# Two PSUM banks each for the scan's scores and outputs, and one merged product for base and routing in a decoder layer

## What is computed

```python
# 1: mixer and MLP            (B, L, D = 8, 128, 512; 4 heads of 128; INTER = 1792)
h   = x + mamba2(rmsnorm(x) * ln1_w)          # in-projection, convolution, scan, out-projection
h2  = rmsnorm(h) * ln2_w
x   = layernorm(x + h + silu(h2 @ gate_w.T) * (h2 @ up_w.T) @ down_w.T)
# the scan of a tile: att = (C @ B.T) * exp(cs_q - cs_k) on q >= k;  y = att @ (X * dt) + D * X;  y * silu(z) @ w_out.T
# 2: attention to ctx
x   = layernorm(x + softmax(x @ ctx.T) @ ctx)
# 3: base product and one of four rank-8 experts
top = argmax(x @ gate_w.T + expert_bias)      # 4 logits for each token
x   = layernorm(x + x @ W_up + lora(x, top))  # lora: A (8 x 512) and B (512 x 8) of the chosen expert
```

## Time and profile before

| | us |
|---|---|
| median of 3 runs (406.89 to 409.05) | 407.15 |
| the profiled execution | 408.65 |
| its span in the trace | 406.8 |
| TensorE busy | 389.2 (96%) |
| VectorE busy | 296.8 (73%) |
| ScalarE busy | 190.8 (47%) |

### The profile page before, as it was taken

One profiled execution on the slowest core, in us unless ns is written; L12 is line 12 of the kernel. 1 busy time (PEld: TensorE's weight loads), 2 busy tenths in 40 slices (PEclk: granted clock), 3 DMA queues, 4 the chain that ended last, 5 costly groups with the idle time before them and its releaser, 6 DMA issues.

```text
span 406.8 us, 5242 instructions
## 1 busy us (share of the span) xinstructions
PE 389.2 (96%) x1856; PEld 311.5 (77%) x1856; DVE 296.8 (73%) x520; ACT 190.8 (47%) x383; POOL 131.4 (32%) x117
## 2 busy tenths in 40 slices
PE   7999999998979999999999999999999999999984
PEld 3778787665669988888888888887888788787753
DVE  2489995257885788979797979695467657665676
ACT  5678457856664656251524244863313234142131
POOL 2504222934334575547372737920000000000000
PEclk9999999998999999999999999999999999999998
DMA  7801530110001014111212111441110120110002
GB/s 272 280 20 52 180 132 2 50 53 0 1 2 44 10 47 162 52 53 52 74 38 97 52 53 52 155 157 52 53 52 26 53 77 26 52 58 21 27 0 77
DMA packets 12834, 27.62 MB, mean 68 GB/s; under 512 B 1825, under 2 KB 1953, under 8 KB 12810
## 3 DMA queue, kind: packets, MB, share of 16 engines
q1 hardware_dynamic: 11658, 25.22, 18.4%
q10 hardware_dynamic: 1152, 2.10, 1.4%
HBM read 25.20 MB, written 2.11 MB: 67 GB/s over the span
## 4 chain that ended last, share of the span: by engine, by line
PE 81%; DVE 8%; ACT 5%; POOL 3%; issue 2%; ACTq 0%; DVEq 0%; POOLq 0%
PE bank L605 23%; PE bank L607 23%; PE bank L606 23%; PE bank L721 2%; PE bank L861 2%; PE bank L872 1%; PE bank L616 1%; PE bank L883 1%; POOL sets L524 1%; PE bank L644 1%; ACT big L1065 1%; PE bank L667 1%; DVE tmp L1695 1%; PE bank L843 1%; DVE big L1486 1%
## 5 line engine op out<-in xcount | busy, mean ns | idle before, releaser
L605 PE MATMUL bank<-sets,station 128*128 128x512 f32 (+1 forms) x424 | 164.2, 387 | 2.0 <-POOL station L482 0.9
L607 PE MATMUL bank<-sets,station 128*128 128x512 f32 (+1 forms) x424 | 158.5, 374 | 0.0
L606 PE MATMUL bank<-sets,station 128*128 128x512 f32 (+1 forms) x424 | 158.4, 374 | 0.0
L605 PEld LDWEIGHTS bank<-sets,station 128*128 128x128 f32 x424 | 80.0, 189 | 20.0 <-issue 3.5
L606 PEld LDWEIGHTS bank<-sets,station 128*128 128x128 f32 x424 | 80.0, 189 | 15.3 <-issue 2.2
L607 PEld LDWEIGHTS bank<-sets,station 128*128 128x128 f32 x424 | 79.8, 188 | 14.3
L563 POOL TENSOR_TENSOR big<-tmp,side_f 128x512 f32<-128x512 f32 x17 | 26.4, 1569 | 23.7 <-DVE side_f L1582 23.7
L482 POOL TENSOR_TENSOR station<-raw,station 128x1024 fp32r<-128x1024 f32 x7 | 16.8, 2400 | 40.0 <-ACT station L982 40.0
L1286 ACT ACTIVATE small<-small 128x1 f32<-128x1 f32 x24 | 7.1, 294 | 48.0 <-DVE small L1697 48.0
L1582 DVE TENSOR_TENSOR side_f<-side_f,bank 128x512 f32<-128x512 f32 x36 | 24.6, 684 | 3.9 <-PE bank L607 3.5
L1443 DVE SCALAR_TENSOR_TENSOR big<-bank,cw,big 128x508 f32<-128x508 f32 (+2 forms) x36 | 26.2, 740 | 1.3 <-ACT big L1042 0.3
(11 more groups left out here) (184 smaller groups left out, 653.8 us busy)
## 6 DMA issues: line engine op xcount, KB each, us to landing
raw<-wstream SPq DMA_DIRECT2D x31, 512.0 KB, 3.3
rows<-x SPq DMA_DIRECT2D x8, 256.0 KB, 4.2
big<-ctxT SPq DMA_DIRECT2D x8, 256.0 KB, 2.6
big<-ctx SPq DMA_DIRECT2D x8, 256.0 KB, 2.9
out<-tmp ACTq DMA_DIRECT2D x8, 256.0 KB, 2.0
decays<-step_rows SPq DMA_DIRECT2D x4, 256.0 KB, 3.6
big<-step_rows SPq DMA_DIRECT2D x4, 256.0 KB, 5.5
big<-ln_w SPq DMA_DIRECT2D x1, 256.0 KB, 5.1
```

Source lines behind the costliest of these rows:

```text
L605: pe.matmul(ps, a_hi, b_lo, start=first, stop=False)
L606: pe.matmul(ps, a_hi, b_hi, start=False, stop=False)
L607: return pe.matmul(ps, a_lo, b_hi, start=False, stop=last)
```

## The change

**Scan.** Scores go to bank 6 for even blocks and 0 for odd ones, y to bank 1 for even and 7 for odd; the waits that guard them refer to block b - 2. `scores_of(b + 2)` stands directly behind `y_of(b)` for all b below 6. The high part of the first y is made by VectorE.

**Down loop.** The 36 routing columns are put ahead of the 512 columns of W_up, and both are multiplied in the three passes of fp32r as 548 columns, in two halves of 274 (banks 7 and 6, 24 matmuls a tile). The 4 products of `route` in plain fp32 and the 12 base matmuls of 512 columns go. ACT makes the high part of x2 straight from PSUM, VectorE the low part from PSUM; the copy of x2 and VectorE's cast go. `lora` becomes two matmuls of 238 and 274 columns, `add_ffn` two additions. VectorE chooses the expert in 7 instructions instead of 8, makes `route` ahead of `split_hid`, and `normed(0)` ahead of `moments(2)`. A segment of `down` stands ahead of `base`. Four more small instructions make the parts of the routing weights once.

**End.** 5 of the 14 k-blocks of `down(7)` (before 8) stand ahead of `turn_x1(6)`; `base(6)` is cut into chunks between the steps of tile 7; the steps behind the last LayerNorms are interleaved anew; tiles 5, 6 and the second half of 7 are stored from the SP queue; the last normalisation is made in two halves.

```diff
-SEGS = ((0, 8), (8, 10), (10, 12), (12, 14))
-END_SEGS = ((0, 8), (8, 9), (9, 10), (10, 11), (11, 14))
+SEGS = ((0, 8), (8, 10), (10, 12), (12, 13), (13, 14))
+END_SEGS = ((0, 5), (5, 6), (6, 8), (8, 9), (9, 13), (13, 14))
...
-                if b >= 1:
-                    pe.wait_ge(att_ok, H * b)
-                pe.matmul(bank[6][:, :], bT[:, tok(b)], cT[:, :, tok(b)], start=True, stop=True).then_inc(s1_done, 1)
+                if b >= 2:
+                    pe.wait_ge(att_ok, H * (b - 1))
+                pe.matmul(score_bank(b)[:, :], bT[:, tok(b)], cT[:, :, tok(b)], start=True, stop=True).then_inc(s1_done, 1)
...
-                if b >= 1:
-                    pe.wait_ge(y_gated, b)
-                else:
+                if b >= 2:
+                    pe.wait_ge(y_gated, b - 1)
+                elif b == 1:
                     pe.wait_ge(z_done, 6)
...
-                if 3 <= b < B - 2:
+                if b < B - 2:
                     scores_of(b + 2)
...
-                if b < 3:
-                    scores_of(b + 2)
...
+            def base_half(h, bk, x2, chunks=range(DC)):
+                cols = (slice(0, PAIR_N), slice(PAIR_N, BASE_N))[h]
+                for c in chunks:
+                    q = bass.ts(c, P)
+                    mm = three_pass(pe, bank[bk][:, 0:PAIR_N], x2[:, 0, q], x2[:, 1, q], base_w(0, c)[:, cols],
+                                    base_w(1, c)[:, cols], c == 0, h == 0 and c == DC - 1)
+                    if h == 0 and c == DC - 1:
+                        mm.then_inc(route_ps, 1)
...
+                base_half(0, 7, x2S)
+                base_half(1, 6, x2S)
...
+                pe.matmul(bank[bks[0]][:, ROUTE:PAIR_N], zmT[:, :], lbS[:, 0:n], start=False, stop=True,
+                          skip_group_check=True)
+                pe.matmul(bank[bks[1]][:, 0:PAIR_N], zmT[:, :], lbS[:, n:D], start=False, stop=True).then_inc(ffn_ps, 1)
...
                     attend(t - 1, 1 - par)
+                if d:
+                    down(t, par, 2, first_d)
                 if f:
-                    route(t - 2)
                     base(t - 2, first_f)
...
-            route(last - 2)
+            turn_x2(last - 1, 0)
+            down(last, 1, 5, False, END_SEGS)
             base(last - 2)
-            turn_x2(last - 1, 0)
-            turn_halves(last, u1, ln_out[0], (2, 0), q_ps)
-            turn_z(last - 2)
+            turn_halves(last, u1, ln_out[0], (2, 5), q_ps)
             attend(last, 1, halves=True)
             lora(last - 2)
+            pe.wait_ge(x2_lo, last)
+            base_half(0, 1, x2_parts[1], (0, 1))
             turn_ex(last)
-            route(last - 1)
+            base_half(0, 1, x2_parts[1], (2,))
             mix(last)
-            base(last - 1)
+            base_half(0, 1, x2_parts[1], (3,))
+            base_half(1, 0, x2_parts[1])
+            keep_warm(4, 4, wd(0, 0)[:, 0:P], wd(0, 0))
             turn_halves(last, u2[:, 1, :], ln_out[1], (3, 5), x2_ps)
-            keep_warm(4, 2, wd(0, 0)[:, 0:P], wd(0, 0))
...
-                if b < B:
+                if 1 <= b < B:
                     hi_of_y(b)
...
+            def hi_of_first_y():
+
+                v.wait_ge(y_gated, 1)
+                v.tensor_copy(yS[:, 0, 0, :], hn[:, 0, :]).then_inc(y_hi, 1)
...
-                    moments(2, t - 3, u3)
                 if a:
                     normed(0, t - 1, u1)
                 if g:
+                    moments(2, t - 3, u3)
                     normed(2, t - 3, u3)
                 if f:
-                    split_x2(t - 2)
+                    lo_of_x2(t - 2)
                 if a:
                     row_max(t - 1)
+                if f:
+                    route(t - 2)
                 if split:
                     split_hid(t + 1, 1 - par)
-                if f:
-                    route(t - 2)
```

More of the change, by code:

```diff
@@ L322, in h2_rows, with score_bank, y_bank @@
             return tmp[:, bass.ds((4 + t - (B - 2)) * D, D)].rearrange("p (g c q) -> p g c q", g=2, c=2)
+        def score_bank(b):
+            return bank[0 if b % 2 else 6]
+        def y_bank(b):
+            return bank[7 if b % 2 else 1]
         def h2_bank(t):
@@ L370, in blocks, with base_w @@
             return ap.rearrange("p (c q) -> p c q", c=DC)
+        def base_w(part, c):
+            return base_end if part * DC + c == 2 * DC - 1 else baseS[:, part * DC + c, :]
         def context(t):
@@ L888, in base @@
+            def base(t, first_use=False):
                 pe.wait_ge(x2_lo, t + 1)
                 if first_use:
-                    pe.wait_ge(bw_lo, 2)
-                elif bk == 6:
+                    pe.wait_ge(bw_lo, 5)
+                else:
                     pe.wait_ge(ln_u[2], t)
[L893 to L899, removed]
@@ L909, in tail, with lora_last @@
+            def lora_last(t):
+                pe.wait_ge(zmT_ok, t + 1)
+                pe.matmul(bank[6][:, :], zmT[:, :], lbS[:, :], start=False, stop=True).then_inc(ffn_ps, 1)
             def tail(t, par, d=True, a=True, f=True, first_d=False, first_f=False):
@@ L926, in tail @@
                 if d:
[L927 removed]
+                    down(t, par, 3, first_d)
                 if f:
@@ L1329, in tail @@
                 if f:
-                    copy_x2(t - 2)
+                    hi_of_x2(t - 2)
+                if split:
+                    split_hid(t + 1, 1 - par, first_split)
                 if g:
@@ L1352, in _ @@
             copy_q(last - 1)
-            copy_x2(last - 2)
+            hi_of_x2(last - 2)
             store(last - 3)
@@ L1356, in _ @@
             rstd(1, last - 1)
+            hi_of_x2(last - 1, x2_parts[1])
             rstd(0, last)
-            copy_x2(last - 1)
-            copy_halves(last, qT, q_ps, (2, 0), q_ok)
-            copy_z(last - 2)
+            copy_halves(last, qT, q_ps, (2, 5), q_ok)
+            copy_z(last - 2, bk=2)
             exp_scores(last)
+            rstd(2, last - 2)
             rstd(1, last)
             copy_halves(last, x2T, x2_ps, (3, 5), x2_ok)
-            copy_z(last - 1)
-            rstd(2, last - 2)
-            store(last - 2)
-            copy_z(last)
+            for i in range(2):
+                act.activation(x2S[:, 0, bass.ts(i, 2 * P)], bank[3 + 2 * i][:, 0:2 * P], ACT.Copy).then_inc(x2_hi, 1)
+            copy_z(last - 1, bk=4)
+            copy_z(last, bk=4)
             rstd(2, last - 1)
             rstd(2, last, slot=0)
-            store(last - 1, u1)
-            store(last, u_last)
+            act.wait_ge(ln_out[2], last + 1)
+            act.dma_start(out[last, :, 0:HALF_K], u_last[:, 0:HALF_K]).then_inc(stored, 16)
         @block.vector
@@ L1810, in _ @@
             add_ffn(last - 3, 0, stored_tiles=last - 3)
+            normed(0, last - 1, u1)
             moments(2, last - 3, u3)
-            normed(0, last - 1, u1)
             normed(2, last - 3, u3)
-            split_x2(last - 2)
+            lo_of_x2(last - 2)
             row_max(last - 1)
```

175 lines of the change are left out of this document (114 added, 61 removed).

## The result

| | before | after |
|---|---|---|
| median, us | 407.99 (4 runs, 406.89 to 409.05) | 402.65 (4 runs, 402.12 to 403.94) |
| profiled execution, us | 408.65 | 402.7 |
| its span, us | 406.84 | 400.90 |
| ratio, after to before | | 0.9874, 95% interval 0.9834 to 0.9915 |

A second set of runs gave 402.81 for the changed kernel beside 408.40 for the kernel before, ratio 0.9875 (0.9854 to 0.9895). The forecast was 402.4 with a range of 400.9 to 405.6.

The account below looks back on a forecast made before the run. TensorE, busy 96% of the span, was taken as the bound, except in the scan, a ring of ScalarE and VectorE; -1.99 + 1.2 - 0.88 - 2.36 - 0.79 + 0.1 = -4.7, from 407.15 to 402.4 us, range 400.9 to 405.6.

Parts of the forecast that it names:

- The chain: Scan: three waits go, from the first y's high part, scores(3) behind out_proj(0), and the residual's wait for out_proj: -1.99 us.
- The clock: Scan: TensorE's idle time gathers into one piece of about 4 us and loses the full clock: +1.2, bounds 0 and 2.2.
- the first y's 0.53: Scan: the first y's high part leaves ScalarE, so the xb copy behind it starts 0.53 us earlier.
- Tile 1: Down loop, tile without base: a down segment covers TensorE's wait for ScalarE's exponentials: -0.88 us.
- Tiles 2 to 5: Down loop, four full tiles: 24 matmuls of 274 columns replace routing and base, 0.59 us a tile: -2.36.
- Rival (a): Down loop: lora's 238 columns run at fp32's pace, +0.3 in six tiles, +1.8, 404.2 us; chance 0.18.
- Rival (c): Down loop: VectorE becomes the bound, possibly with clock loss before turn_x1(6): 404.0 to 405.5 us; chance 0.20.
- rival (d): Down loop: stationary-column loads of 0.189 us pace the short matmuls, +0.87 a tile, 411.2 us; chance 0.04.
- (b): Scan: the clock holds behind the idle time, 1.2 us less, 401.2 us; chance 0.10.
- (e): Scan: second banks help nothing since bank 5 and xb hold blocks together, idle time stays in two portions: 402.7; chance 0.03.
- Tile 6: Last loop tile: fewer down k-blocks ahead, TensorE waits for normed(0), VectorE sets a period of 15.57 us: -0.79.
- End: From turn_x1(6) on: add_mlp(7) 2.04 later, against 0.85, 0.95 and small pieces of 0.15 saved: +0.1, bounds -0.7 and +1.0.

Follow-up runs that it names:

- e4: Changed kernel with the third LayerNorm's moments again ahead of normed(0) in the down loop, not in the hand-written end: 404.52 us, ratio to before 0.9926.
- e5: Changed kernel with split_hid again ahead of route on VectorE: single run, tiles 15.82 us, tile 6 15.22 instead of 15.42; no total given.
- e6: Changed kernel without the down segment between attend and base: single run, tile 1 13.03 us, tile 6 14.53 instead of 15.42, sum unchanged.
- e3: Changed kernel plus 14 matmuls without use in TensorE's scan idle time: 400.86 us, ratio to before 0.9838; scan 37.78 instead of 38.87.
- e1: Changed kernel with the first y's high part back on ScalarE: 403.73 us, ratio to before 0.9915; scan 39.40 instead of 38.87.
- e2: Changed kernel with one bank each for scores and y, old waits and old scores order, first y still on VectorE: 403.12 us, scan 39.89.

## Why the prediction was right

The mechanism was in the main the one forecast in each stretch, and the bounds that were named (TensorE in the four tiles, VectorE in tile 6) are what e4, e5 and e6 show. That the sum agrees so closely, -4.73 from y(0) on for -4.7, is luck: scan, tile 1 and tile 6 gave 0.60 more than forecast, and the four tiles and the end 0.55 less. It is luck as well that the time lies 0.25 from the forecast, which was counted from a median of three runs, 407.15; the median of four is 407.99, and from there the same sum gives 403.3.

**Scan.** The chain was forecast 1.99 shorter. The transposes behind the idle time came at 114.02 before and 110.66 after, each counted from its y(0): 35.03 and 32.88, 2.15 shorter. The third copy of xb was 0.51 earlier (forecast 0.53), the fourth 1.64 (1.58). The clock fell behind an idle time of 4.06 (forecast about 4) and cost 1.09 (1.2, e3). Net -1.06 against -0.8. What was wrong is how the gain was shared out: the first y's 0.53 counts only together with the new banks and order, 0.53 with them (e1) and 0.04 without (e2).

**Tile 1.** -1.07 for -0.88: the wait in brackets in the earlier trace rows counts from a matmul's modelled end, and what comes back is counted in starts. e6 gives the same 1.08, behind the same wait of 0.88.

**Tiles 2 to 5.** -2.17 for -2.36. The term that was mis-sized is the distance of the 274-column matmuls, 0.128 for 0.125: 24 x 0.003 = 0.07, where 0.05 is missing in a tile. The fault lay in the row it was scaled from: three 256-column matmuls gave 0.117, but over the whole first part of gate and up the kernel before starts them 0.120 apart on the mean, and by columns that makes 0.128. VectorE followed with 0.45 between the end of normed(0) and turn_x1, where 0.31 was worked out (0.21 of slack and 0.1 of hand-over); add_attention came 0.28 later (9.83 for 9.55 behind turn_x1) against 0.30, and from there the end of normed(0) came 0.82 earlier against 0.74. That TensorE stayed the bound hung on the new LayerNorm order (e4). Rival (a) fell: 238 columns are followed after 0.11. Rival (c) fell by the 0.45, rival (d) by the 0.128; of the rivals in the scan, (b) fell by the clock of 0.50, (e) by the one idle time of 4.06 and by e2.

**Tile 6.** -0.94 for -0.79, bounded by VectorE as forecast: 15.42 is the tile of 15.82 less a slack of 0.40 (0.45 without the hand-over of 0.05), where 0.21 was worked out. The idle time of 1.49 in front of turn_x1(6) did not cost the clock (1.00 in the windows of 369 to 372 us).

**End.** +0.46 for +0.1, the largest miss. add_mlp(7) came 2.06 later relative to turn_x1(6) (forecast 2.04). From there to attend(7) 0.91 was saved (0.85), from the last normed(1) to the last addition 1.00 (0.95: 394.11 to 401.59 before, 389.12 to 395.60 after). The step that failed lies between: from attend(7) to the last normed(1) the forecast put a share of its small gains of 0.15, and the trace has 6.68 for 6.42, 0.26 more. attend(7) stood before, and stands now, at

```profile
387.69 1.06 PE L861 MATMUL bank<-big,tmp 128*128 128x128 f32 x8
...
382.44 0.94 PE L887 MATMUL bank<-big,tmp 128*128 128x128 f32 x6 [0.26 <-ACT tmp L1363]
```

There the chunks of base(6) stand ahead of mix, and VectorE waits 0.68 for it. Another 0.05 lies behind the last normalisation, in the stores (3.07 for 3.01). These pieces are read from the two traces; no run takes them back one by one.

**Start.** -1.21 that nobody forecast, of the unchanged stage. It is why the profiled executions differ by 5.9 and the stretches from y(0) on by 4.7.

## What to carry to other kernels

Removing work from the bound is worth only as much as the next engine has slack: here the merged product gave nothing in the four tiles until VectorE's order was changed too, so put a number on the second engine's slack before counting the gain. Two waits in series are not two gains: a step that starts earlier and then waits for the same thing has gained nothing. When one engine waits for a second, and soon after the second for the first, move the first one's independent work ahead of its wait.

## What the runs showed of the hardware

A matmul of 36 moving columns with its own load starts 0.111 us behind the one before, one of 274 only 0.128: an eighth of the columns saves only 0.017. An idle TensorE lost its clock behind 1.97 us in one place and not behind 2.04 or 1.49 in others, so the length of the wait alone does not tell it; and behind one and the same 4.06 the half clock began before the next instruction in one execution and behind it in another, with 1.1 us between them. And the first stage, up to y(0), took 77.06 to 79.02 us in profiles of kernels whose code does not differ there, while the later stages repeated within about 0.1, but for the one scan with the longer half clock.
